# A rotary attention's fill: where the first key's split and the third batch's norm stand in three engines' queues

## The reference

```
x = x + attention_a(layernorm(x))     # causal, 16 heads of 8; three heads reweigh their keys
x = x + ffn(layernorm(x))
x = x + attention_b(layernorm(x))     # no mask, 16 heads of 8, rotary positions on q and k
x = x + ffn(layernorm(x))             # the same weights as the first
ffn(x): h = silu(x W1 s1) * (x W2 s2); h = gelu(h H1 g1); h = gelu(h H2 g2); return h W3 s3
rotary: (a, b) -> (a cos - b sin, a sin + b cos) for each pair of features of q and k
```

## Time and profile before

| what | us |
|---|---|
| median of 3 runs (2062.24 to 2064.73) | 2063.32 |
| profiled execution | 2065.22 |
| span of that profile | 2063.5 |
| first attention, about | 0 to 640 |
| first feed-forward layer, about | 620 to 959 |
| fill of the second attention | 901 to 1001 |

### The profile page before, as it was taken

How to read it: one execution, slowest core, us unless ns; L and a number is a source line. 1 busy time by engine, 2 the same in 40 slices (tenths; PEclk the granted TensorE clock), 3 DMA queues, 4 the chain that set the end, 5 groups by cost and what they waited for, 6 DMA issues and landing times.

```text
span 2063.5 us, 42740 instructions
## 1 busy us (share of the span) xinstructions
PE 1888.6 (92%) x16132; PEld 966.2 (47%) x16132; DVE 1702.8 (83%) x2312; ACT 1478.0 (72%) x2641; POOL 1175.8 (57%) x1615
## 2 busy tenths in 40 slices
PE   3899999999889999986899999999999989999998
PEld 1333444444357777764222222222222227777776
DVE  4889898898658888876899999999999918888883
ACT  1478788788756666652698888888888876666665
POOL 6777788877446555677444454454553015555654
PEclk6799999999989999998799999999999989999999
DMA  7455656655110000014334444444444010000000
GB/s 180 99 120 134 131 125 140 126 121 119 25 40 1 0 1 1 1 27 101 88 90 101 99 105 107 95 100 95 101 111 95 14 19 12 11 16 11 11 16 16
DMA packets 107892, 144.81 MB, mean 70 GB/s; under 512 B 19105, under 2 KB 87458, under 8 KB 101538
## 3 DMA queue, kind: packets, MB, share of 16 engines
q1 hardware_dynamic: 107682, 142.01, 30.3%
HBM read 67.52 MB, written 55.58 MB: 60 GB/s over the span
## 4 chain that ended last, share of the span: by engine, by line
PE 59%; POOL 15%; issue 8%; ACT 8%; DVE 6%; DMA 2%; SPq 1%; POOLq 0%; another core or an unknown queue 0%; ACTq 0%; DVEq 0%
PE ps_score L1446 21%; PE ps_out L1065 12%; PE ps_score L1007 7%; ACT prob L993 6%; PE ps_max L1446 5%; PE ps_max L1025 5%; DVE negmax L882 3%; POOL xhat L324 3%; POOL prob L728 3%; PE ps_out L1446 3%; PE ps_max L1106 2%; POOL rstd L318 2%; POOL rest L693 1%; ACT o_raw L956 1%; POOL parts L700 1%
## 5 line engine op out<-in xcount | busy, mean ns | idle before, releaser
L993 ACT ACTIVATE prob<-ps_score 128x512 f32<-128x512 f32 x1664 | 900.4, 598 | 171.8 <-PE ps_score L1007 151.4
L882 DVE TENSOR_REDUCE negmax<-ps_max 128x2 f32<-128x1024 f32 (+1 forms) x896 | 905.6, 1066 | 90.7 <-PE ps_max L1042 47.9
L1065 PE MATMUL ps_out<-prob,v_aug 128*9 128x256 f32 (+2 forms) x6656 | 508.9, 386 | 30.9 <-ACT o_raw L956 20.4
L1446 PE MATMUL ps_score<-h,w_hi 128*128 128x512 f32 x2048 | 502.8, 399 | 9.4 <-POOL h L1224 8.2
L1446 PEld LDWEIGHTS ps_score<-h,w_hi 128*128 128x128 f32 x2048 | 383.3, 189 | 104.3 <-POOL h L1224 10.8
L1025 PE MATMUL ps_max<-stack_k,stack_q 48*128 48x512 bf16 (+3 forms) x2048 | 342.6, 353 | 46.6 <-DVE negmax L882 29.3
L1007 PE MATMUL ps_score<-stack_q,stack_k 50*128 50x512 bf16 (+3 forms) x2048 | 351.6, 347 | 31.0 <-ACT prob L993 23.1
L1212 POOL TENSOR_TENSOR h<-h3f,h 128x512 fp32r<-128x512 f32 x128 | 192.5, 1514 | 127.9 <-ACT h L1358 127.8
L728 POOL TENSOR_SCALAR_AFFINE_SELECT prob<-prob 128x256 f32<-128x256 f32 (+1 forms) x448 | 187.8, 440 | 117.7 <-ACT prob L993 117.3
L1065 PEld LDWEIGHTS ps_out<-prob,v_aug 128*9 128x9 f32 x6656 | 105.8, 89 | 306.0 <-ACT prob L993 153.9
L1007 PEld LDWEIGHTS ps_score<-stack_q,stack_k 50*128 50x128 bf16 x2048 | 103.7, 93 | 273.1 <-ACT prob L993 201.6
(11 more groups left out here) (116 smaller groups left out, 2129.5 us busy)
## 6 DMA issues: line engine op xcount, KB each, us to landing
d_stack<-parts SPq DMA_DIRECT2D x64, 384.0 KB, 2.6
stack_q<-d_stack SPq DMA_DIRECT2D x64, 384.0 KB, 5.7
stack_k<-d_stack SPq DMA_DIRECT2D x64, 384.0 KB, 6.0
d_stack<-parts SPq DMA_DIRECT2D x64, 256.0 KB, 2.9
d_stack<-parts SPq DMA_DIRECT2D x64, 128.0 KB, 2.7
o_num<-o_raw SPq DMA_DIRECT2D x128, 64.0 KB
o_rden<-d_rden SPq DMA_DIRECT2D x128, 64.0 KB
turned<-qf SPq DMA_DIRECT2D x64, 128.0 KB, 2.4
```

Source lines behind the costliest of these rows:

```text
L882: last = dve.tensor_reduce(m["negmax"][:, t, :, p], banks[:, :, at:at + w], AX.X, ALU.max, negate=True)
L993: act.activation(prob(b, i)[:, o], act_bank("score", 2 * i + o), ACT.Exp).then_inc(s["prob"], 1)
L1065: last = pe.matmul(m["ps_out"][32 * g:32 * g + HD + 1, out:out + w], m["v_aug"][b % VALUES][:, j, 4 * G + g, :], prob(b, beat)[:, g % 2, l ...
L1446: mm = pe.matmul(to, w[:, cols], moving(part), start=begin and i == 0, stop=last and i == len(pairs) - 1)
```

## The change

Four places of the fill are touched; nothing is added or left out.

1. POOL, step 14: the four remainders of the third hidden activation go between `high` and `middle_low` of batch 0's q.
2. DVE, step 14: batch 0's k is taken out of PSUM before both splits of h1 instead of between them, and `parts_on_vector` for k goes from before the fourth column's gate and split to behind them.
3. DVE, step 1 of the rotary attention: the statistics of batch 2 go from beat 16 to between beats 4 and 5, ahead of the projection of batch 1's q.
4. POOL, `pool_fill`: the norm of batch 2 goes from behind the parts of batch 1's k to ahead of them.

```diff
@@ pool_fill
         ones(pool, range(1, VALUES))
+        norm(pool, 2)
         high(pool, 1, "k", 1)
         middle_low(pool, 1, 1)
-        norm(pool, 2)
         negated_max_parts(pool, 0, 0)
@@ vector
-                if i == AT["D_stats"]:
+                if i == AT["D_stats"] and not (rotary and n == 1):
                     statistics(dve, n + 1)
@@ pool_layer
             if r == B - 2:
                 low(pool, b, 2, range(FT))
                 fill["high"](pool, 0, "q", 0)
+                low(pool, b, 3, range(FT))
                 fill["middle_low"](pool, 0, 0)
-                low(pool, b, 3, range(FT))
@@ vector_layer
             if fill:
                 fill["project"](dve, 0, "q", 0)
-            split(dve, b + 1, 0)
             if fill:
                 fill["project"](dve, 0, "k", 1)
+            split(dve, b + 1, 0)
             split(dve, b + 1, 1)
...
             split(dve, b + 1, 2)
-            if fill:
-                fill["parts_on_vector"](dve, 0, "k", 1)
             gated(dve, b + 1, 3)
             if r < B - 2:
                 xT_low(dve, b + 2)
             split(dve, b + 1, 3)
+            if fill:
+                fill["parts_on_vector"](dve, 0, "k", 1)
...
         after.vector(dve, 1, 0, 5)
+        fill["statistics"](dve, 2)
         fill["project"](dve, 1, "q", 0)
```

## The result

The changed kernel took 2072.16 us in the median of 8 runs (2068.01 to 2074.42), the kernel before 2063.99 in 8 (2061.22 to 2067.18). The ratio is 1.0038 with a 95% interval of 1.0027 to 1.0049. The forecast was 2066.1 with a range to 2071.0. The direction of the sum was right and its size was not: +8.2 us where +2.8 stood.

What follows compares the result with a forecast made beforehand. PE, busy 92%, was taken as the bound, so only its waits in the fill could give. Beat 3 2.9 us later, less 0.1 for rounding, made 2063.3 + 2.8 = 2066.1 us, range 2060.0 to 2071.0.

Steps and rivals of the forecast that it cites:

- the sum: Whole kernel: beat 3 of step 2 comes 2.9 us later, 0.1 off for rounding, +2.8 us.
- The two waits aimed at: Batch 2's norm: PE waits 3.91 us, DVE then 4.01; step 14: POOL's remainders hold PE's last product until 929.97.
- Step 14: Remainders 2.5 us sooner, but load k of batch 0 lands at 948.9; beat 0 begins 4.4 us later.
- The clock: PE's lower clock after some 7 idle us before beat 0: costs 1.5 us, between nothing and 7 us.
- 5.9: POOL's start on batch 1's q: 4.4 us from beat 0 plus 1.5 us of clock later, at 963.6.
- the slower rival: PE stays at 1.2 GHz from beat 0 through the layer's end: +8.4 us, median 2071.7; chance 0.14.
- The chain from q of batch 1 to beat 3: POOL and SP, batch 1's q to step 2's beat 3: 38.5 us instead of 41.5, at most 3.0 gained.
- start + 38.5: Beat 3 of step 2 from POOL's start on batch 1's q: 17.5 + 3.9 + 3.7 + 0.8 + 1.5 + 11.1 us.
- 3.7 us: SP, batch 1: time from store k to load k once load q has long landed.
- 11.1 us: From the swap of batch 2's q on SP to the end of POOL's L667.
- 92.6: Beat 3 of step 2, counted from batch 0's transposes, by the sum on record for parts 3 and 4 alone.
- 5.4 us along DVE's maxima: Fill, DVE's maxima: 4.0 us from the norm's wait plus 1.4 us from moving the statistics.

Runs made afterwards that it cites:

- experiments 3 and 4: Kernel before with part 1 alone (POOL's remainders): 2070.57 us, ratio 1.0037; kernel before with part 2 alone (DVE's k): 2063.36 us, ratio 0.9999.
- experiment 8: Changed kernel with products that nothing reads on PE ahead of beat 0: with 56, 2070.32 us, ratio 1.0033; with 68, 2069.10 us, ratio 1.0030.
- experiment 10: Changed kernel with batch 0's store k ahead of load q, and maxima's rows and batch 2's swap ahead of batch 1's load k: 2062.80 us, ratio 1.0000.
- Experiment 2: The norm alone: kernel before with parts 3 and 4 (statistics and norm of batch 2 moved), step 14 as before: 2064.87 us, ratio 1.0009.
- experiments 5, 6 and 9: Batch 2's swap ahead of load k: on changed kernel, 1.0016; on kernel before with parts 3 and 4, 0.9984; the latter with maxima's rows ahead too, 0.9980.
- the run with 68 products: Changed kernel with 68 products that nothing reads on PE in the wait before beat 0: 2069.10 us, ratio 1.0030 against the kernel before.

## Why the prediction was wrong, point by point

**What the kernel waits for, right.** The two waits aimed at were real, and the one at beat 19 went in every kernel with the norm's move.

**Step 14, right, and its size too.** Forecast: q's parts stored 25.8 us from the base (929.4), store k to load k 7.8 us, first maximum at 45.3 (948.9) behind a wait of 7 us. Found: 26.05, 7.88, 45.62 and 7.74. The reading that two transfers would collide here, from two pairs of rows at other distances, held; experiments 3 and 4 put the whole of it on POOL's part.

**The clock, right in size.** 1.5 us was taken between bounds of nothing and 7 us, and 1.5 measured by experiment 8. One row for it was misread: 930 to 932, where "the level came back", shows 0.56, and the clock was falling there. POOL's q of batch 1 came 6.3 us later from the base (60.40 against 54.11) where 5.9 stood. In experiment 10 the same work took 5.4 us more at the lower clock, in keeping with the slower rival, but that is not what the changed kernel's profile shows: the rival had q of batch 1 at 65.5 from the base. That its total of 2071.7 lies near the measured 2072.2 is chance.

**The chain from q of batch 1 to beat 3, mis-sized: this is the step that failed.** It was put as "start + 38.5" and measured 42.5 (60.40 to 102.89). Two of its terms carry 3.9 of these 4.0 us. "3.7 us" from store k to load k of batch 1 was 5.29, and the "11.1 us" from the swap to L667's end was 13.4, since the 2.97 us from the swap's issue to POOL's start in it came from a row in which no load was in flight ahead of the swap. The sum itself moved the swap from 7.6 us behind load k to about 2.3 us behind it, and load k takes 6 to 7 us to land. The same collision that I had priced at batch 0 was left out at batch 1. With it the sum would have been 2.8 + 2.3 = 5.1, and with the store's 1.6 us 6.7. Of the 1.5 us that are left to the 8.2 us of the medians, 0.4 is q of batch 1, which began at 60.4 where 60.0 was summed. The profiled pair differs by 7.5 us at the end and by 7.3 at beat 3; the rest, about 0.9 us, stays open, and the runs of the changed kernel alone spread over 6.4 us. Experiment 2 shows the mistake without step 14: the formula's 92.6 against 95.58, and experiments 5, 6 and 9 take the collision away by order alone.

**The statistics, wrong without effect.** Of the 5.4 us along DVE's maxima 1.4 stood for the statistics, and the rows of experiment 2 show that they were already hidden behind PE's projection of v: 3.9 us is what the norm's move can give. The sum did not rest on it, since POOL's chain was the later one.

**The store's extra 1.6 us, not foreseen.** Between the issue of store k and load k of batch 1 an instruction fetch may run on the transfer engines. The transfers of the changed kernel by queue, 984.2 to 989.8 (packets, MB, share of the 16 engines), show one:

```profile
q8 instruction: 1, 0.02, 1.2%
```

The same question to nine traces splits them: with such a fetch in the stretch the step took 4.13, 4.20, 4.37, 4.42, 5.12, 5.27 and 5.29 us (the kernel before is the 4.42), without one 3.71 and 3.72 (the norm alone, and the run with 68 products). In the changed kernel the last of the three transfers of store k landed after 4.3 us, in the run with 68 products after 2.8. No run moved the fetch alone, so this is a correspondence in nine of nine and not a shown cause.

## What to carry to other kernels

Before a piece of work is moved ahead of another, follow what the other feeds through every queue up to the next wait of the busy engine: here 3.9 us gained at one beat came back as 3.9 us at another, and two blocks exchanged on POOL delayed a store at the head of SP's queue by 6 us. A piece of work taken out of a busy engine's queue gives time only if nothing else fills its place: the statistics stood beside a projection on PE and gave none. When issues move closer together, the time of a transfer is no longer the one in the old trace: price it from a row in which the transfer ahead is as near, or as a full wait for it. And small urgent transfers belong ahead of big ones in the issuer's queue; that order alone turned a change worth nothing (1.0009) into one worth 0.16 to 0.20%, which is little but clear of the intervals.

## What the runs showed of the hardware

A swap (two transfers of 128 KB) issued 2.35 us behind a load of 768 KB took 5.25 to 5.79 us until its reader started (five traces), and 2.91 to 2.98 us with no load in flight ahead (eight traces). A store of 768 KB took until the load that waits for it 7.6 to 8.0 us with another load of 768 KB issued 0.84 us ahead (six traces), 5.68 with 3.06 and 6.14 with 3.04 us, and 3.70 with 5.65 us ahead. The work from the first maximum to q of batch 1 took 13.2 us with the clock kept up, by products which nothing reads or because there was no stop. With the clock down it took 14.7 to 15.3 us in five traces. After the same stop of 4.5 us it took 15.9 us in one kernel, where the clock was back 8 us behind the first maximum, and 18.6 in another, where it was back only 15 us behind it; what decides this was not tested.
